# Low parts of 28 expert weight tiles moved from VectorE to GpSimd

## What is computed

```python
h = gelu(einsum('td,edh->eth', xf, W1) + b1)        # 8 experts, 512 -> 2048
expert_out = einsum('eth,ehd->etd', h, W2) + b2      # 2048 -> 512
out = einsum('etd,te->td', expert_out, weights)      # weights: softmax over the two best of 8
```

## Time and profile before

| what | value |
|---|---|
| times of three runs | 1742.57 us median, 1740.15 to 1744.72 |
| the profiled execution's own time | 1737.34 us |
| its span, first to last instruction | 1735.5 us |
| PE (matmul) busy | 1642.4 us, 95% of the span |
| DVE busy | 880.4 us, 51% |
| ACT busy | 695.5 us, 40% |
| POOL busy | 306.2 us, 18% |
| mean granted TensorE clock | 0.974 of full |

### The profile page before, as it was taken

The page is one execution under the profiler, slowest core; times in us unless marked ns, Lnnn a source line. Parts: engine busy times, 40 slices in busy tenths (PEclk is TensorE's granted clock), DMA queues, the critical chain, the costliest instruction groups (busy, mean ns, idle before and its releaser), DMA issues. The chain is left out here.

```text
span 1735.5 us, 26943 instructions
## 1 busy us (share of the span) xinstructions
PE 1642.4 (95%) x10858; PEld 1384.9 (80%) x10858; DVE 880.4 (51%) x1592; ACT 695.5 (40%) x1314; POOL 306.2 (18%) x257
## 2 busy tenths in 40 slices
PE   7999999999999999999999987994999999999886
PEld 6888888888888888888888766773888888888885
DVE  4344443443344434443443575785777457558842
ACT  5333333333333333333333433453655345345621
POOL 4201210011101110111010061465321011011101
PEclk9999999999999999999999998996899999999898
DMA  6601820111011101111002460113757337437711
GB/s 230 220 6 53 132 73 7 53 56 53 12 48 56 53 23 37 56 53 37 26 4 80 144 198 25 51 57 128 257 160 218 125 94 229 157 87 237 218 33 21
DMA packets 54070, 165.17 MB, mean 95 GB/s; under 512 B 10580, under 2 KB 10964, under 8 KB 53376
## 3 DMA queue, kind: packets, MB, share of 16 engines
q1 hardware_dynamic: 38032, 131.88, 22.3%
q0 software_dynamic: 15888, 31.19, 8.5%
HBM read 143.54 MB, written 55.64 MB: 115 GB/s over the span
## 5 line engine op out<-in xcount | busy, mean ns | idle before, releaser
L405 PE MATMUL psum<-ctx,Wk 128*128 128x512 f32 x1536 | 384.9, 399 | 0.0
L405 PE MATMUL psum<-Wv,ctx 128*128 128x512 f32 x1536 | 368.7, 389 | 0.0
L405 PEld LDWEIGHTS psum<-Wv,ctx 128*128 128x128 f32 x1536 | 288.3, 188 | 59.7
L405 PEld LDWEIGHTS psum<-ctx,Wk 128*128 128x128 f32 x1536 | 279.3, 188 | 55.4
L887 DVE SCALAR_TENSOR_TENSOR kT<-psum,bkc,kT 128x512 fp32r<-128x512 f32 x128 | 96.0, 750 | 387.9 <-ACT kT L1251 387.9
L405 PE MATMUL psum<-xgT,Wh 128*128 128x224 f32 (+5 forms) x1536 | 249.8, 316 | 13.4 <-issue 13.4
L405 PEld LDWEIGHTS psum<-xgT,Wh 128*128 128x128 f32 x1536 | 228.5, 196 | 30.6 <-issue 15.6
L746 PE MATMUL psum<-Wh,hs 128*128 128x512 f32 x1008 | 250.3, 394 | 0.5 <-DVE hs L1139 0.5
L746 PEld LDWEIGHTS psum<-Wh,hs 128*128 128x128 f32 x1008 | 185.1, 189 | 35.2 <-DVE hs L1139 0.9
L1251 ACT ACTIVATE kT<-psum,bkc 128x512 fp32r<-128x512 f32 x128 | 88.3, 690 | 247.6 <-PE psum L405 247.5
L1416 ACT ACTIVATE gl<-psum,b1c 128x512 f32<-128x512 f32 x128 | 87.7, 686 | 205.8 <-PE psum L405 205.7
(11 more groups left out here) (146 smaller groups left out, 1770.1 us busy)
## 6 DMA issues: line engine op xcount, KB each, us to landing
raw<-in_W SPq DMA_DIRECT2D x128, 512.0 KB, 3.8
expert_rows<-in_spare_rows SPq DMA_DIRECT2D x16, 1042.0 KB, 7.4
raw<-in_ctxT SPq DMA_DIRECT2D x32, 512.0 KB, 4.4
xg<-expert_rows POOLq DMA_DIRECT2D x32, 256.0 KB, 5.5
low_parts<-Olo POOLq DMA_DIRECT2D x32, 128.0 KB, 2.4
oT<-low_parts SPq DMA_DIRECT2D x8, 512.0 KB, 4.6
out_x<-x SPq DMA_DIRECT2D x12, 256.0 KB, 2.0
xs<-in_x SPq DMA_DIRECT2D x4, 512.0 KB, 6.6
```

The source lines that it names most:

```text
L405: mm = pe.matmul(dst, l, r, start=n == 0, stop=n == len(pairs) - 1)
```

## The change

Of jobs 1 to 7, the low parts of tiles 1, 5, 9 and 13 (28 tiles, just those that go through `raw[3]`) are made by GpSimd. Its job body has them between `fetch_rows(q + 1)` and the scatters of job q: first tile 13 of job q, then tiles 1, 5 and 9 of job q+1. VectorE leaves them out.

```diff
+        def on_gpsimd(q, i):
+
+            return q % E != 0 and i % 4 == 1
...
-                    if i > LAG and more:
+                    if i > LAG and more and not on_gpsimd(q + 1, i - LAG - 1):
                         split_low(q + 1, i - LAG - 1)
-                    if i <= LAG and q % E:
+                    if i <= LAG and q % E and not on_gpsimd(q, NI + i - LAG - 1):
                         split_low(q, NI + i - LAG - 1)
...
             def job(q, width, more):
                 if more:
                     fetch_rows(q + 1)
+                for i in range(NI - LAG - 1, NI):
+                    if on_gpsimd(q, i):
+                        split_lo(w_load(q, i), Wh[i][1][:], Wh[i][0][:])
+                for i in range(NI - LAG - 1):
+                    if more and on_gpsimd(q + 1, i):
+                        split_lo(w_load(q + 1, i), Wh[i][1][:], Wh[i][0][:])
                 g.wait_ge(meta_in[q % 2], 16 * (q // 2 + 1))
```

## The result

The changed kernel takes 1781.5 us (median of 4 runs, 1780.4 to 1784.8) against 1743.6 us for the kernel before (4 runs, 1740.2 to 1750.5): 1.0209 times, 95% interval 1.0183 to 1.0235. That is 37.9 us more, where 30 had been forecast. Repeated later beside 17 more runs of the kernel before it was 1777.9 us (4 runs) against 1742.3, 1.0196 (1.0144 to 1.0248).

The account below looks back on a forecast made before the run. PE was taken as the bound. Stops in jobs 1, 3, 5 and 6 summed to 24.9 us; with (a) -2.9, (b) +4.8 and (c) +3.0 that made 29.8 us on 1742.6, so 1772 us, range 1755 to 1788.

Parts of the forecast that it names:

- What bounds the kernel: PE bounds the expert part (job 2: 89.07 of 89.10 us); work taken off DVE is not by itself time.
- Tile 13: Its low part on POOL stands behind scatters' landing and six fetches; the late load stops PE, 24.9 us over four jobs.
- R: Time at which POOL's subtraction for tile 13 frees `raw[3]` in a narrow job; 1443.79 in job 3.
- correction (a): Scatters in jobs 1, 3, 5 land sooner beside one load, so the buffer is freed earlier: -2.9 us (0 to -9).
- The second group of transposes: PE's turning of chunk 1 in narrow jobs waits for chunk 0's low part: 8.0 us later in job 3.
- The loads behind the first: Loads of tiles 2 and 3, behind tile 1's in narrow jobs, take 2.33 us each and land at R + 8.9.
- correction (b): POOL and DVE keep each other out when subtracting in SBUF: 1.2 us in each of four jobs, +4.8 (0 to 9.6).
- some 55 us: Length expected for job 3 in the changed profile, instead of 47.6 us.
- (c): PE's clock halves after idles in jobs 1, 3 and 5: 1 us a job, +3 us (0 to 15).
- The lock binds in every narrow tile: Rival: DVE and POOL never subtract at once, slowing each narrow tile; +41 us, 1783 us, chance 0.13.
- No change: Rival: release reaches ACT before PE needs it, or POOL makes tile 13 in slot 1; 1742.6 us, chance 0.05.
- faster: Rival: DVE's relief in job 6 removes the 4.14 us idle and half clock; -9 us, 1733 us, chance 0.05.

Follow-up runs that it names:

- the pair with tile 13 only: GpSimd makes only tile 13's low part, against the kernel before: behind the fetches 1765.0 us, ahead of the wait for the scatters' landing 1744.4 us.

## Why the prediction came out right

The difference was 37.9 us where the sum had 29.8; the mechanism held, and the terms fit less well than the total in the range suggests.

**What bounds the kernel.** Right. The wide jobs did not move by 0.1 us in the first profile. DVE's relief was worth nothing that was measured: no kernel with fewer subtractions on VectorE was faster than the kernel before.

**Tile 13.** Right in mechanism: the place on POOL alone makes 21 us or 0 (the pair with tile 13 only), and a bare wait on SP does the same. The steps for job 3, from the job's start: R forecast at 1443.8 - 1421.9 = 21.9 us, measured 21.0, 0.9 earlier, where correction (a) took 1.2. The second group of transposes was forecast 8.0 us later than before and came at 33.5 against 25.7 us, 7.8 later.

That agreement is in part luck: it holds two errors that cancel. The loads behind the first were taken to land 2.33 us apart, the pace of job 3 before; ACT found tiles 2 and 3 with no wait, 1.5 us apart. So the high part of tile 3 ended 8.1 us after R, not 9.9. The pace of a stream in which each load waits for a buffer is not the pace of loads that are free to go.

In return the way from there to the transposes took 4.5 us, where the sum with correction (b) had 3.1. The sum let VectorE begin the low part of tile 3 as soon as its high part was done (at 1463.59). VectorE began it at 1466.12: it was busy without a break from the cast of gelu(6) at 1461.15 on, with the gelu results of two slots and the low part of tile 2. So the second stop was set by gelu(6), that is by the load of tile 1, and then by VectorE's own queue, and not by the loads of tiles 2 and 3. It was so with tile 13 alone, too: tile 3's high part was done at 1458.85, its low part begun at 1460.07, VectorE busy without a break from 1455.66. Of the 4.5 us, and of the stop, 1.7 us are the held-up cast, for which (b) had 1.2; the cast held up to 2.42 us lies behind the chunk.

The last paragraph's "some 55 us" for job 3 does not fit the sum's own 9.0, which gives 56.6; measured in the same way, without the gap ahead of job 4, it took 57.0.

**The sum by jobs.** With the corrections it had 7.9, 9.0, 8.7 and 4.1 us for jobs 1, 3, 5, 6; measured 9.6, 9.1, 9.5, 10.0, and in the repetition 8.7, 8.9, 8.8, 5.8. The term that was too small is job 6. No clock cost was put down there under (c), and in the first profile the granted clock was 0.50 from its first matmul for 37.5 us. With the clock at full at its start the loss was 5.8 us, 2.7 of them up to the second group of transposes. In job 3 the clock was half from about 1461 to 1471; most of it lay under the second stop, as forecast, and after the transposes only about 1.2 us more were lost.

**Not foreseen.** 2.4 and 2.7 us in job 7 and the end, where the changed kernel does only one more thing on GpSimd. Nearly all of it is the end itself: from the start of POOL's last scatter to the end of the span it takes 15.1 us (15.3 again) instead of 12.8. The third kernel with all 28 subtractions, the one with tile 13 ahead of the wait, has 15.8; all the others, also those with 21 of them, have 12.8 to 13.0. So it goes with the full set of 28 and not with any one tile. What it is was not tried. The 3.2 us ahead of job 1 are not certain to be part of the change: the repetition has 0.9, and 58 runs of the kernel before spread from 1733.8 to 1757.3 us.

**The rivals.** "The lock binds in every narrow tile" fell: with the 21 subtractions of tiles 1, 5, 9 the kernel loses 5 us, and with all 28 and tile 13 early job 3 takes 48.2 us. It fell as the main cost; 13 us stay in that kernel, and the lock may have a part in them. Tile 1 on POOL costs one to two microseconds where DVE is already late, and the 1.7 us of the held-up cast in job 3 are of that size. That VectorE's operation is held up until POOL's subtraction is over is shown by the rows above (the cast ended 0.28 us after it), and it fits what the Trainium skill, page "SBUF — State Buffer", section "SBUF: two separate sides", states: an exclusive lock, held for the whole instruction. The trace agrees: 2.12 against 0.42 us for a cast, 3.76 against 1.22 us for a subtraction. A cast can lose more than POOL's 2.4 us: in job 4 of the changed kernel one took 3.76 us, from 1503.26, during POOL's last fetches, to 0.30 us after its subtraction; at 448 tokens it cost nothing. "No change" and "faster" needed R five to twelve microseconds earlier; moved ahead of the wait, tile 13 alone gave the first and not the second, as it would with DVE's relief off the path.

## What to carry to other kernels

An operation moved to an idle engine inherits that engine's queue: look not at how busy it is but at what stands ahead of the operation in its order, and where the operation's result was due. In a ring of buffers with loads issued in order, one late release stops every load behind it, and a chain of in-order engines then hands the stop on; whether it costs depends on the time that one tile of the bound engine covers (nothing at 5.3 to 5.6 us a tile, 6 us a job at 2.5 to 3). The hand-on is not only the wait itself: VectorE had 21 us of work without a break behind the stop in job 3, and the second stop came out of that backlog. If such work is to go to another engine, put it ahead of that engine's long waits. Here that made the move harmless for tile 13 alone; nothing made it a gain, since VectorE did not bound the kernel.

## What the runs showed of the hardware that was not expected

The same kernel ran job 6 in 60.1 us with the granted clock at 0.50 for its first 37.5 us, and in 55.9 us with job 6 begun at full clock. The idle ahead of the job was 2.98 us in the one and 1.29 us in the other; in the other profiles of this study idles of 0.4 to 1.4 us there were followed by full clock, 1.7 to 3.0 us by half clock. At the start of job 2 an idle of 2.77 us was not followed by half clock in two profiles, while at the start of job 4 idles of 2.87 and 2.91 us were, so the idle ahead of the job alone does not decide it. In job 6 the granted clock was then 0.50 to 0.55 for 24 to 37.6 us, in the wide job 4 it was 0.54 and 0.67 for 5 to 7. What makes that idle longer was not tried.
